# Expert mixtures of a two-layer network on one core: three of four row-block stores issued by ScalarE, a PSUM copy moved to VectorE, half of the in-loop sums moved behind the loop

## What is computed

```
x = x + 0.5 * _L0_ffn_ref(_layernorm(x), ...)
x = x + _L0_attn_ref(_layernorm(x), ...)
x = x + 0.5 * _L0_ffn_ref(_layernorm(x), ...)
x = x + 0.5 * _L1_ffn_ref(_layernorm(x), ...)
x = x + _L1_attn_ref(_layernorm(x), ...)
x = x + 0.5 * _L1_ffn_ref(_layernorm(x), ...)
```

```
x2 = _layernorm(src, ln2_g, ln2_b)
sel = sigmoid(x2 @ sel_w)
scores, idx = top_k(sel, 4)
gate = (one_hot(idx, 32) * scores[..., None]).sum(-2)
h = relu(einsum('bsd,edh->bseh', x2, keys))
moe_out = einsum('bseh,ehd,bse->bsd', h, values, gate)
return src + moe_out
```

## Time and profile before

| | |
|---|---|
| median of 3 runs | 2983.11 us (2978.63 to 2986.97) |
| the profiled execution | 2984.08 us, its span 2982.3 us, mean granted TensorE clock 0.925 |
| PE busy | 2400.8 us (81%) |
| DVE busy | 1943.8 us (65%) |
| POOL busy | 1728.0 us (58%) |
| ACT busy | 1627.8 us (55%) |
| `f4m`: first load issued, first fetch of each sort, last fetch | 1443.7; 1571.6 and 1675.86; 1755.5 us |
| `f6m`: first fetch of each sort, last fetch | 2794.1 and 2893.88; 2973.0 us |

### The profile page before, as it was taken

One profiled execution on the slowest core, in us unless ns is written; L12 is line 12 of the kernel. 1 busy time (PEld: TensorE's weight loads), 2 busy tenths in 40 slices (PEclk: granted clock), 3 DMA queues, 4 the chain that ended last, 5 costly groups with the idle time before them and its releaser, 6 DMA issues. The chain is left out here.

```text
span 2982.3 us, 62217 instructions
## 1 busy us (share of the span) xinstructions
PE 2400.8 (81%) x20200; PEld 1967.5 (66%) x20200; DVE 1943.8 (65%) x4826; ACT 1627.8 (55%) x4697; POOL 1728.0 (58%) x2342
## 2 busy tenths in 40 slices
PE   7999797899799999998466329998999999966650
PEld 5888565688677777777466316666877777756640
DVE  5554586455379899998334347775888999953342
ACT  2332353333288888887222116776988888843220
POOL 4324663432167888888206565554688888841356
PEclk9999898999899999999799759998999999989985
DMA  3930563830122222222345445542222222314552
GB/s 111 362 124 2 131 139 86 344 136 1 29 45 49 56 58 58 58 58 95 89 117 159 106 98 113 108 98 47 44 57 58 57 58 58 114 39 128 141 144 62
DMA packets 278142, 286.14 MB, mean 96 GB/s; under 512 B 34259, under 2 KB 243411, under 8 KB 270643
## 3 DMA queue, kind: packets, MB, share of 16 engines
q1 hardware_dynamic: 261442, 248.58, 30.4%
q0 software_dynamic: 16384, 33.59, 4.0%
HBM read 111.85 MB, written 165.87 MB: 93 GB/s over the span
## 5 line engine op out<-in xcount | busy, mean ns | idle before, releaser
L2783 ACT ACTIVATE f4a_pr<-f4a_sr,f4a_nm 128x256 f32<-128x256 f32 x512 | 239.3, 480 | 29.6 <-DVE f4a_nm L2849 29.3
L2783 ACT ACTIVATE f6a_pr<-f6a_sr,f6a_nm 128x256 f32<-128x256 f32 x512 | 239.4, 480 | 26.7 <-DVE f6a_nm L2849 26.4
L2982 POOL TENSOR_TENSOR f4a_rr<-f4a_tmp 128x256 f32<-128x256 f32 x256 | 194.0, 760 | 90.9 <-DVE f4a_tmp L2857 86.9
L2982 POOL TENSOR_TENSOR f6a_rr<-f6a_tmp 128x256 f32<-128x256 f32 x256 | 193.4, 757 | 83.7 <-DVE f6a_tmp L2857 79.4
L2009 DVE TENSOR_REDUCE a_nm<-a_sr 128x2 f32<-128x512 f32 x256 | 166.9, 685 | 69.9 <-PE a_sr L1742 68.7
L2857 DVE TENSOR_TENSOR f4a_tmp<-f4a_ur,f4a_turn 128x512 f32<-128x512 f32 x256 | 174.8, 683 | 52.1 <-PE f4a_ur L2640 40.2
L2857 DVE TENSOR_TENSOR f6a_tmp<-f6a_ur,f6l_turn 128x512 f32<-128x512 f32 x256 | 174.8, 683 | 45.4 <-PE f6a_ur L2640 33.2
L3286 POOL DMA_INDIRECT f6m_back<-slots,f6o_row x128 | 121.8, 952 | 134.5 <-DMA slots<-f6m_y 96.1
L2655 PE MATMUL f6a_sr<-f6l_pe_hi,f6a_rr_hi 128*128 128x256 f32 x512 | 189.0, 369 | 0.0
L2849 DVE TENSOR_REDUCE f4a_nm<-f4a_sr 128x2 f32<-128x512 f32 x256 | 174.8, 683 | 21.5 <-PE f4a_sr L2657 21.3
L2849 DVE TENSOR_REDUCE f6a_nm<-f6a_sr 128x2 f32<-128x512 f32 x256 | 174.8, 683 | 21.5 <-PE f6a_sr L2657 21.2
(11 more groups left out here) (597 smaller groups left out, 8273.0 us busy)
## 6 DMA issues: line engine op xcount, KB each, us to landing
slots<-f_zero SPq DMA_DIRECT2D x136, 512.0 KB, 6.1
f4m_xr<-slots SPq DMA_DIRECT2D x192, 64.0 KB
slots<-f4m_y SPq DMA_DIRECT2D x192, 64.0 KB
f6m_xr<-slots SPq DMA_DIRECT2D x192, 64.0 KB
slots<-f6m_y SPq DMA_DIRECT2D x192, 64.0 KB
r_scratch<-r_parts SPq DMA_DIRECT2D x32, 192.0 KB, 2.3
all_qs<-r_scratch SPq DMA_DIRECT2D x16, 384.0 KB, 4.8
all_ks<-r_scratch SPq DMA_DIRECT2D x16, 384.0 KB, 6.7
```

The source lines that it names most:

```text
L2783: last = nc.scalar.activation(pr[:, n % 4, x, :], sr.bank(b, n)[:, x * T:(x + 1) * T], ACT.Exp, bias=nm[:, n % SB, x:x + 1], accum_out=zs[ ...
L2982: nc.gpsimd.tensor_tensor(rr[:, hs % RAW, :], tmp[:, hs % 2, 0, :], tmp[:, hs % 2, 1, :], ALU.add)\
```

## The change

Three things change in `mixture`:

- Of the four stores of a round, tiles 0 to 2 (`SPLIT` is 3) are issued by ACT, in a new `store` that loads the four row registers itself. SP issues tile 3 alone. In iteration r ACT stores round r-4 (`LAG` is 4), after take_x(r).
- The copy of `t_ps` to `ht` is DVE's: `take_turned(r-2)` between take_hidden(r-1) and take_y(r-3). ACT's `take_h` is gone.
- Four sums (`MIXED`) stand in the loop in place of eight, at iterations 33, 37, 41 and 45. The other twelve follow behind the loop, in `f4m` behind `then.vector`.

```diff
-    LATE = B - 1
+    LATE, SPLIT, LAG = B - 1, 3, 4
...
+        MIXED = [PER + 9 + 4 * i for i in range(4)]
...
             def store(r):
                 sp.wait_ge(y_ready, r + 1)
-                for n in range(QUARTET):
+                for n in range(SPLIT, QUARTET):
                     sp.dma_start(w.slots[bass.ds(rows[r][n], P), :], y[:, r % YB, n, :]).then_inc(y_out[r % YB], 16)
...
-            def take_h(r):
-                act.wait_ge(h_turned, r + 1)
-                if r >= 2:
-                    act.wait_ge(y_made, r - 1)
-                nc.scalar.activation(ht[:, r % 2, :], t_ps[:, :], ACT.Copy).then_inc(ht_ready, 1)
+            def store(r):
+                rows = registers(nc.scalar, "row", r, 0)
+                act.wait_ge(y_ready, r + 1)
+                for n in range(SPLIT):
+                    nc.scalar.dma_start(w.slots[bass.ds(rows[n], P), :], y[:, r % YB, n, :]).then_inc(y_out[r % YB], 16)
...
-            for r in range(ROUNDS + 2):
+            for r in range(ROUNDS + LAG):
                 if r < ROUNDS:
                     take_x(r)
-                if r >= 2:
-                    take_h(r - 2)
+                if r >= LAG:
+                    store(r - LAG)
...
+            def take_turned(r):
+                dve.wait_ge(h_turned, r + 1)
+                if r >= 2:
+                    dve.wait_ge(y_made, r - 1)
+                nc.vector.tensor_copy(ht[:, r % 2, :], t_ps[:, :]).then_inc(ht_ready, 1)
...
                 if 0 <= r - 1 < ROUNDS:
                     take_hidden(r - 1)
+                if 0 <= r - 2 < ROUNDS:
+                    take_turned(r - 2)
                 if r >= 3:
                     take_y(r - 3)
                 late(r)
-                if r >= PER + 8 and (r - PER) % 2 == 0 and (r - PER - 8) // 2 < BEFORE:
-                    mix((r - PER - 8) // 2)
+                if r in MIXED:
+                    mix(MIXED.index(r))
...
-            for i in range(BEFORE, B):
+            for i in range(len(MIXED), B):
                 mix(i)
```

## The result

The changed kernel takes 2902.51 us (median of 4 runs, 2901.33 to 2908.16), the kernel before beside it 2983.2 (4 runs, 2978.63 to 2986.97): a ratio of 0.973, 95% interval 0.9715 to 0.9753. Forecast were 2901 us. Two later comparisons gave ratios of 0.972 and 0.973; the three differences of the medians are 80.7, 83.6 and 82.0 us.

A forecast was written before the change was run, and what follows sets the result against it. SP's issuing of loads and stores was taken to bound the loop, with POOL's fetches behind it. Gains of 60.4 + 19.4 + 2.9 = 82.7 us from 2984.08 gave 2901 us, range 2882 to 2946.

The forecast's parts named there:

- T: Time of one round of the mixture's loop, forecast to fall from about 4.67 to 3.25 us.
- The 0.22 for long issues: SP's unusually long issues add 0.22 us a round to 2.91, if they go with the number of issues (5 of 8).
- the 2.64 counted: ACT's work a round: take_x 0.78, a register load 0.51 and three stores 1.35, in all 2.64 us.
- The rival of the issues that exclude each other: SP's and ACT's issues in the loop don't run side by side: T = 4.0, gain 34 us, 2950 us; chance 0.13.
- Part 1, the first sorts: Rounds 6 to 28 in both mixtures: 22 x (4.67 - 3.25) less 1 us is 30.2, twice 60.4 us gained.
- the 1 us for `late` steps: Deduction of 1 us in each first sort for DVE's `late` steps, which had room before.
- t0: Start of POOL's first fetch of a mixture's first sort, forecast to keep its 5.9 us distance to load 28.
- Part 2, the second sort of `f6m`: POOL, not the stores, is late next: fetches start at t0 + 80.4 in place of t0 + 99.8, 19.4 us gained.
- Part 3, the second sort of `f4m`: Fetch 16 waits for a sum behind the forerun, moving from t0 + 104.3 to t0 + 101.4: 2.9 us gained.
- Part 4, everything behind keeps its length: 64 fetches in 80 us, last sums and output stay; twelve sums behind the loop, 26 us of DVE, lie under POOL's fetches.
- No jitter: Rival: all limits met in the loop, T = 2.95, 98 us gained, 2886 us; chance 0.06.
- the closed loop: Rival: jitter and DMA latency give T = 3.6 to 3.8; at 3.7, 56.5 us gained, 2928 us; chance 0.17.
- the slower one: Rival: ACT becomes the bound through costlier stores; at 1.25 us each T is 5.25, 68 us slower, 3052; chance 0.04.

The follow-up runs named there:

- the four kernels: The kernels run on the slower chip: changed kernel with all stores on SP, copy on ACT, four stores on ACT, six sums; ratios 1.009, 0.9878, 0.9845, 0.9793.

## Why the prediction was right, and what in it was wrong

**The bound.** Right. SP's issuing set the round, and taking three issues from it took the gain of the first sorts: with them back a round of these is about 1 us longer on the same chip, and with a fourth taken they get shorter still.

**The round.** T was forecast as 3.25 and is 3.25 on average (3.19 to 3.35). SP's floor of 2.91 is 2.88. The 0.22 for long issues came out nearly as a number, but not by its reason. Issues of SP over 0.46 us were 11 in the rounds 6 to 47 of `f4m` before, 11.3 us over the usual length in all, 0.28 a round; they are 12 now, 9.7 us, so 0.24. Their count did not fall to 5 of 8: only the single one got shorter. What is left of T, some 0.13, is what I called jitter. In the rounds 6 to 46 SP's store begins 0.16 us a round later behind the loads than the usual 0.09 in `f4m`, and 0.09 in `f6m`: these are its waits for the copy of `y` (18.9 us in `f4m` with those at the loop's end, where it was 1.7). PE's wait for loaded rows was forecast below 30 us and is 40.7: a miss, since 21.2 of it stand ahead of the first round. DMA shares and rates, forecast 0.60 at 175 and 0.8 at 214 GB/s, are 0.60 at 170 and 0.78 at 208.

**ACT's price.** Right: 0.34 us a store, the lower bound, and the issues begin under the activation, so that ACT had more room than the 2.64 counted. The rival of the issues that exclude each other falls by the same rows: both engines issue at once, and no median duration changes by more than ACT's 0.02 us. The lock that the Trainium skill describes ("Perfetto Trace Analysis", section "DMA Instruction — HWDGE (DVE, Sync)") shows in these durations as those 0.02 us at most. The Trainium skill's other sentence, that issuing from several engines saves only the sequencer's time, which is usually small ("DMA: Bandwidth & Descriptors", section "Issuing engines are not separate DMA queues"), holds in its first half: what SP's issues shrank by (4.33 to 2.88 us a round) is about what the round shrank by. Here that was not small: it was most of the round.

**Part 1, the first sorts**, forecast 60.4, measured 64.8 (30.9 and 33.9). T in `f4m` was higher and in `f6m` lower than 3.25; the 1 us for `late` steps didn't show, and t0 followed load 28 by 5.6 and 5.8 us.

**Part 2, the second sort of `f6m`**, forecast 19.4, measured 15.0. POOL is late next, as said, and does run from one sort into the other, without a wait. But one fetch took 4.94 us:

```profile
2797.05 0.94 POOL L3295 DMA_INDIRECT f6m_back<-slots,f6o_row  x1 [0.30 <-DVE all_x L3228]
2798.30 4.94 POOL L3295 DMA_INDIRECT f6m_back<-slots,f6o_row  x1 [0.30 <-issue]
...
2796.04 6.38 DVE L3228 SCALAR_TENSOR_TENSOR all_x<-f6m_back,f6o_half,all_x 128x128 f32<-128x128 f32 x24
```

again ending 0.8 us behind the end of a row of sums. That is 4.0 of the 4.4 us missing.

**Part 3, the second sort of `f4m`**, forecast 2.9 gained, measured 1.6 lost. The mechanism stood: the forerun's step at t0 + 80.3 (80.5 forecast), fetch 16 at t0 + 100.3 (101.4), so 4.0 us sooner than before. What was missing is again the long fetch, 6.0 us.

**Part 4, everything behind keeps its length**: this is the step that failed, in the sentence that the twelve sums behind the loop lie "under POOL's fetches". They lie beside them and hold them: 6.0 and 4.0 us. The total came out right because 4.4 us more from the first sorts and 4.5 from the stretch between and the start made up for the 8.9 us missing in the second sorts; a part of that agreement is luck.

**The rivals.** No jitter (2886) and the closed loop (2928) are excluded by the measured T, the slower one by ACT's 0.34 us a store. Seven sums and four stores on ACT together were not tried.

## What to carry to other kernels

When one queue's issues bound a loop, count them and move them to an engine that has room. Then look at what was placed by the old pace. Sums that wait for fetches had to move from every second to every third round because the rounds got faster, and moving more than that put 16 us of waiting behind another part. Long rows of DVE work on operands in SBUF should not stand where POOL's indirect fetches are the bound: single sums of 2.2 us, spread among the fetches, made none longer than 1.27 us.

## What the runs showed of the hardware

**A row of sums on DVE holds a fetch of POOL.** Where DVE runs `scalar_tensor_tensor` on SBUF operands in a row of 4.3 us or more, a fetch that starts well inside the row is held to its end. The traces of twelve executions have 24 such fetches, which start 2.25 to 4.34 us into the row. All of them end 0.81 to 0.88 us after its end, after 1.46 to 13.20 us (rows of 4.3 to 14.8 us). The 14 fetches that start up to 1.46 us into such a row take 0.94 to 1.09. Copies from PSUM didn't hold one. Single sums of 2.2 us do the same on a small scale: the two fetches of 1.27 us in the kernel before, one in each mixture, start 1.73 us into a sum and end 0.82 after it. The Trainium skill ("SBUF — State Buffer", section "Who interferes with whom") says that a DVE instruction with two SBUF inputs contends with a GpSimd instruction that reads SBUF, and infers of `tensor_tensor` that it doesn't hold the generation of descriptors. The first half fits these rows. The inference, carried over to `scalar_tensor_tensor`, would have these fetches go through, and here one was held for up to 13.2 us; which part of an indirect fetch is held, the reading of its row numbers or the making of its descriptors, no run here shows. Why fetches pass that start early in a row is open, too.

**Long issues come with transfers of instructions.** Around 1513 both engines are slow at once, SP's four loads with 3.36 us in place of 1.89 (the timeline above) and ACT's three stores with 3.23 in place of 1.37:

```profile
1512.20 3.23 ACTq L3182 DMA_DIRECT2D slots<-f4m_y  x3
```

The DMA view of 1512 to 1515.9 has a packet of instructions in it (queue: packets, MB, share):

```profile
q8 instruction: 1, 0.02, 2.7%
```

There are about ten such packets in the rounds of `f4m` with either kernel (19 us apart before, 14 now): their number stayed when the time shrank, so they go with the instructions that the program runs, and a faster loop meets them more often. In rounds 6 to 46 of `f4m` all 11 long issues before, and all 18 of SP and ACT together now, overlap in time with such a packet, of this queue or of a second one (q14), and of the 309 ordinary issues now only 20 do. This fits with the number of long issues not having fallen. That the long issues stand beside such packets is seen; that the packets cause them was not tested.

**Chips differ.** On the slower chip a register move of SP took up to 0.72 us where it takes at most 0.05 on the other, in stretches in which many of SP's instructions took some 0.70 us (four loads from 1617.70 on took 5.76). SP's register moves ahead of its loads (ns, min/median/max), with six sums in the loop, there:

```profile
L3074 SPq MOVE f4m_xr<-slots x192: 3/29/717, 1444.1 to 1682.6; - x192
```

and in the changed kernel on the other chip:

```profile
L3074 SPq MOVE f4m_xr<-slots x192: 29/29/47, 1443.0 to 1599.1; - x192
```

These stretches lengthen the loop, but they are not what makes the second sorts so slow there (6.4 to 7.1 us a round in the four kernels, where the first sorts take 3.7 to 4.9). The waits of the kernel with six sums between 1440 and 1700 have

```profile
PE f4m_h_ps L3117 <- issue: 25.2, 5, 19.9
...
SPq L3079 <- DVE f4m_y L3212: 57.9, 22, 19.6
```

PE stands idle for 19.9 us (from 1577.1 to 1597.1) with nothing in the trace that it waits for, ACT and DVE stand idle beside it, and SP waits for the copy of `y` that comes late. POOL alone goes on with one fetch in 1.25 us. Each of the four kernels has such stretches in the second sort of `f4m`, the first within 11 us of the first fetch. Gaps of over 3 us in PE's weight loads add up to 46 to 54 us there, of 121 to 135. Without them a round would take 4.7 us with all stores on SP and 3.6 to 4.1 in the others, close to their first sorts (4.9, and 3.7 to 4.0). The changed kernel on the other chips has no gap over 3 us. So SP's issues alone don't set the rounds of the second sorts on the slower chip, and the totals from it say little of the change. What makes PE's gaps and SP's stretches stays open.
